# GAT and mean aggregation on one core: one signal for each store of first products, and the first loads of u issued one group later

## Chip, core and metric

The kernel runs on 1 core of one Trainium2 chip. The metric is the time of one execution on the device, in microseconds; less is better.

## What is computed

There are N = 8192 nodes with C = 64 features and a dense 0/1 adjacency matrix of int32 (8192 x 8192, 256 MB). The first block is a normalization, two graph attention layers and a linear layer over the concatenation; the second is a normalization and a mean over the neighbours.

```python
def _gat_layer(h, adj_mask, W_l, lw, lb, a):
    Wh = h @ W_l
    u = Wh @ lw[:C] @ a
    v = Wh @ lw[C:] @ a
    e = leaky_relu(u + v.T + lb @ a, negative_slope=0.2)
    att = softmax(where(adj_mask, e, -9e15), axis=1)
    return elu(att @ Wh)

h0 = maximum(layernorm(x), 0)                      # h = h0
for i in range(2):
    h = 0.2 * h0 + 0.8 * _gat_layer(h, adj > 0, W[i], lin_w[i], lin_b[i], attn[i])
x = x + concatenate([h0, h1, h2]) @ mlp_w + mlp_b
h = maximum(layernorm(x), 0)
a = (adj == 1)
x = x + concatenate([a @ h / a.sum(1), h], 1) @ weight + bias1
```

## The kernel before

**The mathematics as the kernel lays it out.** exp(leaky_relu(u + v)) is, on either side of the kink, a product of a factor of the row and one of the column. So attention becomes two matrix products over 0/1 masks: an on-mask (edge present, u + v positive) and an off-mask (edge present, u + v not positive), each against h times a column factor, split into bf16 or fp16 parts. The masks are bytes read by TensorE as fp8.

**Tiling.** The adjacency is cut into 64 blocks n = 8 g + c: g is a group of 1024 rows, c a chunk of 1024 columns. A block comes in two loads m = 2 n and 2 n + 1 of 2 MB each (line 285, on SyncE's queue, into 3 buffers); VectorE's conversion m (line 852, `convert`) turns load m from int32 into codes, then packs four columns into a byte (lines 859 and 866), TensorE transposes the packed codes (line 1495), ScalarE takes them from PSUM (line 468) and stores them in DRAM (line 472, `codes_d`), so that the second attention layer and the mean need not read the adjacency again. Load m is issued when conversion m - 3 is done.

**Units.** A block has four units; unit U = 256 l + 4 n + q, with l the attention layer and q one of the four bit places. For each unit ScalarE writes two ramps (line 460, `ramps`) from the row of u (buffer `ub`) into `onb[U % 8]`, VectorE makes the on-mask in place (line 830) and the off-mask in `offb[U % 6]` (line 840), and TensorE multiplies both (lines 1505 and 1511). VectorE runs three blocks ahead with its conversions; inside block n its order is written out by hand: on-mask 0, on-mask 1, off-mask 0, conversion 2 (n + 3), off-mask 1, on-mask 2, conversion 2 (n + 3) + 1, off-mask 2, and so on, in the first group with a part of the split of the next chunk's h in between. Conversions 0 to 5 stand ahead of block 0.

**The start.** Before block 0, for each group k of rows, TensorE multiplies h0 with the weights (line 1463), ScalarE takes h W into `hw` (line 425) and h0 times the first part of `mlp_w`, the first products, into `m0[k]` (line 426), and VectorE takes v and u (line 644). The eight buffers `m0[k]`, 2 KB for each partition, lie in the memory of the mask rings: `m0[0]` to `m0[5]` in `offb[0]` to `offb[5]`, `m0[6]` and `m0[7]` in `onb[6]` and `onb[7]`. They must be in DRAM (`m0_d`) before a mask is written there.

**GpSimd's queue** issues the stores and small loads in program order. `store_u(k)` (line 322) writes the 1024 values of u of group k to DRAM, 4 KB in pieces of 8 bytes; `load_u(k)` (line 329) reads them back to all 128 partitions (512 KB) and first waits until the store of u of that parity has landed; line 345 stores `m0[k]`; `load_h0` (line 335) loads h0. An issuing engine that waits holds back all that stands behind it in its queue.

**The waits in question.** `m0_st` is one semaphore that every store of first products raises by 16 when it lands. Before unit 0's off-mask VectorE waits for 128, and before unit 6's ramps ScalarE does, which is for all eight.

Of the kernel before, what the change touches and what calls it, by code (L numbers as in the profile page):

```python
# [32 lines left out]
NG = N // RG  # L33
# [19 lines left out]
NA, NP, NS, NO = 3, 4, 8, 6  # L53
# [3 lines left out]
def word(bits):  # L57
    return bits * 0x01010101


def w32(buf):
    return buf.bitcast(U32)
# [24 lines left out]
def gnn_program(nc, x, adj, w, lin_w, lin_b, attn, mlp_w, mlp_b, w1, bias1, out):  # L87
    ctx = ExitStack()
    with ctx:
# [3 lines left out]
        def sem(name):  # L93
            return ctx.enter_context(nc.semaphore(name))
# [4 lines left out]
        m0_d = nc.dram_tensor("m0_d", (P, T * C), FP32).ap()  # L99
# [51 lines left out]
        def at(off, n, dt):  # L151
            return region[:, off:off + n].bitcast(dt)
# [8 lines left out]
        m0 = [at(78 * KB + 2 * ((k + 2) % 8) * KB, 2 * KB, FP32).rearrange("p (t c) -> p t c", c=C) for k in range(NG)]  # L161
# [35 lines left out]
        def grp(k):  # L197
            return slice(IT * k, IT * k + IT)
# [4 lines left out]
        def dgrp(d, k):  # L203
            return d.rearrange("p (t c) -> p t c", c=C)[:, grp(k), :]

        def pairs(ap):
            return ap.rearrange("p (q b) c -> p q (b c)", b=2)
# [15 lines left out]
        s_cen, s_sq, hn_r, hi0_r, cat0_r, h0_st = (sem("centred"), sem("squares"), sem("h0_ready"), sem("h0_high"), sem("h0_split"),  # L223
                                                   sem("h0_stored"))
        h_r, hi_r, cat_r = sem("h_ready"), sem("h_high"), sem("h_split")
        m0_st, m_st = sem("m0_stored"), [sem(f"m1_stored{i}") for i in range(2)]
        tT, hT_r, mm_done, mm_out, mm_v, d_r = (sem("h_transposed"), sem("ht_ready"), sem("products"), sem("products_taken"),
                                                sem("products_taken_by_vector"), sem("v_u_ready"))
        u_r, bv_r, w_first = sem("u_ready"), sem("v_scaled"), sem("first_tiles_split")
# [37 lines left out]
        with nc.Block() as block:  # L267
# [35 lines left out]
            def _(pool):  # L303
# [15 lines left out]
                def store_u(X):  # L319
                    l, k = X // NG, X % NG  # L320
                    pool.wait_ge(u_r, 3 * X + 3 if l == 0 else 2 * NG + X + 1)
                    pool.dma_start(u_v[l, k], vu[:, 1, grp(k)].rearrange("p (q b) -> p q b", b=2)).then_inc(u_st[X % 2], 16)  # L322

                def load_u(G):
                    pool.wait_ge(u_st[G % 2], 16 * 4 if 2 <= G < NG else 16 * (G // 2 + 1))
                    if G >= 2:
                        pool.wait_ge(sgn, 4 * NCH * (G - 1))
                    l, g = G // NG, G % NG
                    pool.dma_start(ub[G % 2][:, :], u_d[l, g * RG:(g + 1) * RG].partition_broadcast(P)).then_inc(ub_in[G % 2], 16)

                def load_h0(E):
                    pool.wait_ge(h0_st, 16 * 4)
                    if E >= 2:
                        pool.wait_ge(h_r, E - 1)
                    pool.dma_start(hg[E % 2][:, :, :], dgrp(h0_d, E % NG)).then_inc(hg_in[E % 2], 16)
# [3 lines left out]
                    pool.dma_start(h0_d.rearrange("p (t c) -> p t c", c=C)[:, quarter(k), :], hn[:, quarter(k), :]).then_inc(h0_st, 16)  # L339
                for k in range(NG):  # L340
                    store_u(k)
                    if k < 2:
                        load_u(k)
                    pool.wait_ge(mm_out, 3 * k + 3)
                    pool.dma_start(dgrp(m0_d, k), m0[k]).then_inc(m0_st, 16)
                load_h0(0)
                load_h0(1)
                for e in range(NG):
# [11 lines left out]
                def load_x(e):  # L360
                    if e == 0:
                        pool.wait_ge(d_r, 2 * NG)
                        pool.wait_ge(m0_st, 16 * NG)
                        for i in range(2):
                            pool.wait_ge(m_st[i], 16 * NG // 2)
                    else:
                        pool.wait_ge(xm_r, e)
                    pool.dma_start(pairs(xi[e % 2]), xin_v[e]).then_inc(xi_in[e % 2], 16)
                    pool.dma_start(xg[0], dgrp(m0_d, e)).then_inc(xg_in[0], 16)
                    pool.dma_start(xg[1], dgrp(m1_d, e)).then_inc(xg_in[1], 16)  # L370

                def store_base(e):
                    pool.wait_ge(base_r, e + 1)
                    pool.dma_start(dgrp(base_d, e), x2b[e % 2]).then_inc(base_st[e % 2], 16)

                load_x(0)
                for e in range(NG):
                    if e + 2 < NG:
                        load_u(NG + e + 2)
                    if e >= 2:  # L380
                        store_base(e - 2)
                    if e + 1 < NG:
                        load_x(e + 1)
                    if e + 2 < NG:
                        load_h0(NG + e + 2)
# [10 lines left out]
            def _(act):  # L396
# [45 lines left out]
                def ramps(l, n, q):  # L442
                    U = LU * l + 4 * n + q
                    g, c = n // NCH, n % NCH
                    G = NG * l + g
                    if U >= NS:
                        act.wait_ge(on_done, U - NS + 1)
                        act.wait_ge(off_r, U - NS + 1)
                    elif U == NS - 2:
                        act.wait_ge(m0_st, 16 * NG)  # L450
                    if q == 0 and c == 0:
                        act.wait_ge(ub_in[G % 2], 16 * (G // 2 + 1))
                    if q == 0 and g == 0 and l == 0:
                        act.wait_ge(bv_r, 1)
                    if q == 0 and g == 0 and l == 1:
                        act.wait_ge(d_r, NG + c + 1)
                    sv = onb[U % NS].rearrange("k (i b) -> k b i", b=2)
                    for b in range(2):
                        t = c * TC + 2 * q + b
                        last = nc.scalar.activation(sv[:, b, :], ub[G % 2][:, :], ACT.Relu, bias=bigv[l][:, t:t + 1], scale=BIG)  # L460
                    last.then_inc(sgn, 1)
# [66 lines left out]
                for n in range(NT):  # L528
                    g, r = n // NCH, n % NCH
                    ramps(0, n, 0)  # L530
                    if g == 0 and r > 0:
                        cast_high(0, r)
                    ramps(0, n, 1)
                    if n + 1 < NT:
                        take_codes(n + 1)
                    if r == 5 and g > 0:
                        high(NG + g - 1)
                    ramps(0, n, 2)
                    if n + 1 < NT:
                        store_codes(n + 1)  # L540
                    if g == 0 and r > 0:
                        cast_middle(0, r)
                    ramps(0, n, 3)
                    if g > 0 and r == 7:
                        products(NG + g - 1, 0, tpb)
                    if g > 1 and r < 2:
                        products(NG + g - 2, r + 1, tpb)
                    if g > 0 and r == 0:
                        scaled_sums(g - 1)
                    if g > 0 and r == 3:  # L550
                        row_exp(g - 1)
                    if g > 0 and r == 6:
                        take_ht(NG + g - 1, tpb)
# [32 lines left out]
            def _(dve):  # L586
# [246 lines left out]
                def off_mask(l, n, q):  # L833
                    U = LU * l + 4 * n + q
                    if U >= NO:
                        dve.wait_ge(off_done, U - NO + 1)
                    elif U == 0:
                        dve.wait_ge(m0_st, 16 * NG)
                    dve.wait_ge(on_r, U + 1)
                    nc.vector.scalar_tensor_tensor(w32(offb[U % NO]), w32(pt[(NT * l + n) % NP]), word(BITS[q]), w32(onb[U % NS]),  # L840
                                                   ALU.bitwise_and, ALU.bitwise_xor).then_inc(off_r, 1)
# [178 lines left out]
                for n in range(NT):  # L1020
# [5 lines left out]
                    on_mask(0, n, 0)  # L1026
                    on_mask(0, n, 1)
                    off_mask(0, n, 0)
                    if n + 1 < NCH:
                        split_rest(0, n + 1)  # L1030
                    if ahead:
                        convert(n + 3, 0)
                    off_mask(0, n, 1)
                    if g > 0 and r == 1:
                        add_pairs(g - 1)
# [17 lines left out]
                    if n == 1:  # L1053
                        h_spread(0)
                    off_mask(0, n, 2)
                    if g > 0 and r == 1:
                        lonely_add(g - 1)
# [731 lines left out]
```

## Time and profile before

| What | Value |
|---|---|
| median of 3 runs | 1750.88 us (1749.9 to 1751.87) |
| the profiled execution's own time | 1752.64 us |
| its span | 1750.7 us |
| mean granted TensorE clock | 0.971 of full speed |
| busy, share of the span | TensorE 88%, weight loads 85%, VectorE 88%, ScalarE 73%, GpSimd 5% |
| DMA | 356.01 MB, mean 203 GB/s |

Busy shares are a mean over stages with different limits: up to about 850 us the adjacency is read and the first attention layer runs; then the second attention layer, up to about 1500 us; then the mean over neighbours. Times of instructions count from the span's start. In the timeline "x4" is four instructions merged into one row, and the bracket at a row's end is the idle time before it and what ended it. A time to landing runs from a DMA's issue to its last signal. "DMA share" is the mean busy share of the 16 DMA engines; it can read slightly over 1.

### The profile page before, as it was taken

The page shows a single profiled execution, that of the slowest core. Times are in us where ns is not written, and L with a number is a line of the kernel's source. Part 1 is how long each engine was busy: PE and PEld are TensorE (multiplying, and loading weights), DVE is VectorE, ACT ScalarE, POOL GpSimd, SP SyncE. Part 2 cuts the span into 40 slices and gives each one's busy share as a digit, 9 for nine tenths or more (in the row PEclk, how much of TensorE's full clock was granted, in tenths as well). Part 3 has the DMA queues.
Part 4 walks back from the last instruction along what each step waited for, and adds up shares of the span by engine and source line. Part 5 has one row for each costly group of instructions (what it writes and reads, how often), then busy time and mean ns, then how long its engine had stood idle before and what let it go on. Part 6 is the DMA issues. An engine that isn't in the chain of part 4 may idle for free. (4 is left out here: it accounts for less than half of the span.)

```text
span 1750.7 us, 50197 instructions
## 1 busy us (share of the span) xinstructions
PE 1534.7 (88%) x21779; PEld 1489.1 (85%) x21779; DVE 1533.0 (88%) x2473; ACT 1274.4 (73%) x1411; POOL 89.7 (5%) x124
## 2 busy tenths in 40 slices
PE   2358888888988888888779999999999999799998
PEld 2257778888878878787779999999999999799998
DVE  7789999999999999999788877879688788986665
ACT  3758798989888888889689999999999994000000
POOL 1300000101000010101010000000000000000000
PEclk9679999999999999999889999999999999999999
DMA  7988999999999999998121211122121111233231
GB/s 275 286 306 322 375 364 396 348 410 372 409 385 392 388 384 403 361 410 303 54 51 44 56 43 56 44 68 62 38 62 48 52 54 27 62 116 86 88 93 42
DMA packets 114876, 356.01 MB, mean 203 GB/s; under 512 B 9184, under 2 KB 17376, under 8 KB 114656
## 3 DMA queue, kind: packets, MB, share of 16 engines
q1 hardware_dynamic: 91040, 304.27, 46.5%
q0 software_dynamic: 9152, 29.43, 6.2%
q10 hardware_dynamic: 14464, 19.11, 3.3%
q8 instruction: 171, 2.80, 0.7%
q14 instruction: 49, 0.40, 0.1%
HBM read 325.45 MB, written 27.33 MB: 202 GB/s over the span
## 5 line engine op out<-in xcount | busy, mean ns | idle before, releaser
L460 ACT ACTIVATE region<-ub,bigv 128x1024 uint8<-128x1024 f32 x1024 | 1096.0, 1151 | 38.9 <-PE bank L1511 11.2
L1505 PE MATMUL bank<-wsplit,region 128*128 128x195 bf16 x8192 | 786.5, 250 | 43.9 <-DVE region L830 35.6
L1505 PEld LDWEIGHTS bank<-wsplit,region 128*128 128x128 fp8e3 x8192 | 693.2, 99 | 56.3 <-DVE region L830 37.2
L1511 PE MATMUL bank<-wsplit,region 128*128 128x130 f16 x8192 | 556.4, 221 | 66.7 <-DVE region L840 65.2
L1511 PEld LDWEIGHTS bank<-wsplit,region 128*128 128x128 fp8e3 x8192 | 499.3, 98 | 93.0 <-DVE region L840 89.1
L840 DVE SCALAR_TENSOR_TENSOR region<-region 128x512 uint32<-128x512 uint32 x512 | 338.7, 681 | 22.7 <-DMA m_d<-region 13.3
L830 DVE SCALAR_TENSOR_TENSOR region<-region 128x512 uint32<-128x512 uint32 x512 | 334.4, 681 | 10.8 <-ACT region L460 10.7
L852 DVE TENSOR_SCALAR region<-region 128x4096 uint8<-128x4096 int32 x128 | 292.1, 2282 | 0.6 <-DMA region<-in_adj 0.6
L1718 PE MATMUL bank<-wsplit,region 128*128 128x129 f16 x4096 | 243.5, 222 | 11.1 <-DVE region L1337 11.1
L1718 PEld LDWEIGHTS bank<-wsplit,region 128*128 128x128 fp8e3 x4096 | 241.4, 99 | 12.4 <-DVE region L1337 12.3
L1337 DVE TENSOR_SCALAR region<-region 128x512 uint32<-128x512 uint32 x256 | 100.2, 423 | 43.0 <-PE bank L1718 37.6
L468 ACT ACTIVATE region<-bank 128x1024 uint16<-128x1024 uint16 x64 | 65.9, 1030 | 38.2 <-PE bank L1495 38.2
L859 DVE SCALAR_TENSOR_TENSOR region<-region 128x1024 uint32<-128x1024 uint32 x64 | 77.7, 1214 | 0.0
L1495 PE MATMUL bank<-identb,region 128*128 128x128 bf16 x512 | 40.6, 224 | 24.7 <-DVE region L866 14.6
L1463 PE MATMUL bank<-w,hT 128*128 128x130 f16 (+2 forms) x512 | 36.7, 222 | 20.1 <-ACT hT L417 11.6
L1495 PEld LDWEIGHTS bank<-identb,region 128*128 128x128 bf16 x512 | 32.4, 100 | 25.3 <-DVE region L866 14.9
L1463 PEld LDWEIGHTS bank<-w,hT 128*128 128x128 f16 x512 | 30.2, 102 | 22.3 <-issue 12.5
L322 POOL DMA_DIRECT2D u_d<-vu x16 | 14.2, 889 | 662.8 <-DVE vu L662 658.1
L1326 DVE SCALAR_TENSOR_TENSOR region<-region 128x512 uint32<-128x512 uint32 x64 | 43.7, 682 | 0.0
L866 DVE SCALAR_TENSOR_TENSOR region<-region 128x512 uint32<-128x512 uint32 x64 | 43.5, 680 | 0.1
L903 DVE TENSOR_REDUCE parts<-bank 128x130 f32<-128x390 f32 x36 | 20.0, 563 | 26.3 <-PE bank L1505 24.1
L495 ACT ACTIVATE po<-po 128x512 f32<-128x512 f32 x16 | 10.0, 627 | 42.9 <-DVE po L952 42.7
(193 smaller groups left out, 677.2 us busy)
## 6 DMA issues: line engine op xcount, KB each, us to landing
region<-in_adj SPq DMA_DIRECT2D x128, 2048.0 KB, 10.9
region<-codes_d SPq DMA_DIRECT2D x128, 256.0 KB, 2.7
codes_d<-region ACTq DMA_DIRECT2D x64, 256.0 KB, 6.3
ub<-u_d POOLq DMA_DIRECT2D x16, 512.0 KB, 8.2
hg<-h_d POOLq DMA_DIRECT2D x16, 256.0 KB, 6.3
stg<-m_d POOLq DMA_DIRECT2D x16, 256.0 KB, 5.0
region<-in_x SPq DMA_DIRECT2D x4, 512.0 KB, 6.8
h_d<-wsplit POOLq DMA_DIRECT2D x4, 512.0 KB, 4.2
```

Of the source, the lines that this page charges most:

```text
L460: last = nc.scalar.activation(sv[:, b, :], ub[G % 2][:, :], ACT.Relu, bias=bigv[l][:, t:t + 1], scale=BIG)
L468: nc.scalar.activation(pt[n % NP].bitcast(U16), tpb[:, :].bitcast(U16), ACT.Copy).then_inc(p_in, 1)
L830: nc.vector.scalar_tensor_tensor(on, on, word(BITS[q]), w32(pt[(NT * l + n) % NP]), ALU.bitwise_and, ALU.bitwise_and).then_inc(on_r, 1)
L840: nc.vector.scalar_tensor_tensor(w32(offb[U % NO]), w32(pt[(NT * l + n) % NP]), word(BITS[q]), w32(onb[U % NS]), ALU.bitwise_and, ALU.bitw ...
L852: nc.vector.tensor_scalar(code[:, 4 * h:4 * h + 4, :], adjb[m % NA], 1.375, 3.0, ALU.mult, ALU.min).then_inc(coded, 1)
L859: nc.vector.scalar_tensor_tensor(cq[:, :, :, 0, :], cq[:, :, :, 1, :], 2, cq[:, :, :, 0, :], ALU.logical_shift_left, ALU.bitwise_or).then_ ...
L1337: nc.vector.tensor_scalar(w32(onb[V % NS]), w32(xb[i % 2]), word(BITS[q]), None, ALU.bitwise_and).then_inc(eq, 1)
L1463: last = nc.tensor.matmul(pb[:, k * width:(k + 1) * width], ht[:, it * P:(it + 1) * P], rhs(j), start=(k == 0 and j == 0), stop=(j == 1), ...
L1495: last = nc.tensor.transpose(tpb[:, :].bitcast(BF16)[:, it * P:(it + 1) * P], src[:, it, :], identb[:, :])
L1505: return nc.tensor.matmul(acc_on[it], columns(onb[U % NS], it, b), wsplit[:, c * TC + 2 * q + b, 0:WC], start=(c == 0 and q == 0 and b == ...
L1511: return nc.tensor.matmul(acc_off[it], columns(offb[U % NO], it, b), woff[:, c * TC + 2 * q + b, WO:WO + WF], start=(c == 0 and q == 0 and ...
L1718: last = nc.tensor.matmul(acc_m[g % 2][it], columns(onb[V % NS], it, b), wf16[:, c * TC + 2 * q + b, :], start=(first and b == 0 and it % ...
```

## The change

The one semaphore for the stores of first products becomes eight, one for each store. Before unit U's first use of its ring buffer there is now a wait for store U alone: on VectorE for units 0 to 5 (off-masks), on ScalarE for units 6 and 7 (ramps). Where GpSimd waited for all eight before it reads them back, `load_x(0)`, it waits for each in turn. The two first loads of u leave their place between the store of u and the store of products of groups 0 and 1; they now stand at the end of groups 1 and 2.

```diff
@@ -223,7 +223,7 @@
         s_cen, s_sq, hn_r, hi0_r, cat0_r, h0_st = (sem("centred"), sem("squares"), sem("h0_ready"), sem("h0_high"), sem("h0_split"),
                                                    sem("h0_stored"))
         h_r, hi_r, cat_r = sem("h_ready"), sem("h_high"), sem("h_split")
-        m0_st, m_st = sem("m0_stored"), [sem(f"m1_stored{i}") for i in range(2)]
+        m0_st, m_st = [sem(f"m0_stored{k}") for k in range(NG)], [sem(f"m1_stored{i}") for i in range(2)]
         tT, hT_r, mm_done, mm_out, mm_v, d_r = (sem("h_transposed"), sem("ht_ready"), sem("products"), sem("products_taken"),
                                                 sem("products_taken_by_vector"), sem("v_u_ready"))
         u_r, bv_r, w_first = sem("u_ready"), sem("v_scaled"), sem("first_tiles_split")
@@ -339,10 +339,10 @@
                     pool.dma_start(h0_d.rearrange("p (t c) -> p t c", c=C)[:, quarter(k), :], hn[:, quarter(k), :]).then_inc(h0_st, 16)
                 for k in range(NG):
                     store_u(k)
-                    if k < 2:
-                        load_u(k)
                     pool.wait_ge(mm_out, 3 * k + 3)
-                    pool.dma_start(dgrp(m0_d, k), m0[k]).then_inc(m0_st, 16)
+                    pool.dma_start(dgrp(m0_d, k), m0[k]).then_inc(m0_st[k], 16)
+                    if 1 <= k < 3:
+                        load_u(k - 1)
                 load_h0(0)
                 load_h0(1)
                 for e in range(NG):
@@ -360,7 +360,8 @@
                 def load_x(e):
                     if e == 0:
                         pool.wait_ge(d_r, 2 * NG)
-                        pool.wait_ge(m0_st, 16 * NG)
+                        for k in range(NG):
+                            pool.wait_ge(m0_st[k], 16)
                         for i in range(2):
                             pool.wait_ge(m_st[i], 16 * NG // 2)
                     else:
@@ -446,8 +447,8 @@
                     if U >= NS:
                         act.wait_ge(on_done, U - NS + 1)
                         act.wait_ge(off_r, U - NS + 1)
-                    elif U == NS - 2:
-                        act.wait_ge(m0_st, 16 * NG)
+                    elif U >= NO:
+                        act.wait_ge(m0_st[U], 16)
                     if q == 0 and c == 0:
                         act.wait_ge(ub_in[G % 2], 16 * (G // 2 + 1))
                     if q == 0 and g == 0 and l == 0:
@@ -834,8 +835,8 @@
                     U = LU * l + 4 * n + q
                     if U >= NO:
                         dve.wait_ge(off_done, U - NO + 1)
-                    elif U == 0:
-                        dve.wait_ge(m0_st, 16 * NG)
+                    else:
+                        dve.wait_ge(m0_st[U], 16)
                     dve.wait_ge(on_r, U + 1)
                     nc.vector.scalar_tensor_tensor(w32(offb[U % NO]), w32(pt[(NT * l + n) % NP]), word(BITS[q]), w32(onb[U % NS]),
                                                    ALU.bitwise_and, ALU.bitwise_xor).then_inc(off_r, 1)
```

## Rows read from the trace of the kernel before

**Rows 1.** Long stretches: busy of PE, PEld, DVE, ACT, POOL; PEclk, DMA share, GB/s.
```profile
96.00:846.00 750.00, 643.24 (x8588) 604.67 (x8587) 748.10 (x885) 651.65 (x760) 28.12 (x25) 0.98 0.96 367
...
900.00:1450.00 550.00, 548.63 (x7815) 548.19 (x7813) 448.82 (x830) 522.40 (x501) 27.00 (x38) 1.00 0.18 52
```
**Rows 2.** VectorE's waits from 96 to 860 us: in total, times, longest.
```profile
DVE region L852 <- DMA region<-in_adj: 0.6, 1, 0.6
```
**Rows 3.** Waits of all engines up to 130 us: in total, times, longest.
```profile
DVE region L840 <- DMA m_d<-region: 13.3, 1, 13.3
...
ACT region L460 <- DMA m_d<-region: 10.3, 1, 10.3
```
**Rows 4.** Timeline of VectorE and ScalarE, 58 to 111 us: start, duration, engine, line.
```profile
58.94 0.48 DVE L644 TENSOR_SCALAR vu<-bank,wsc 128x6 f32<-128x6 f32 x3
...
64.96 2.28 DVE L852 TENSOR_SCALAR region<-region 128x4096 uint8<-128x4096 int32 x1
...
65.49 4.25 ACT L460 ACTIVATE region<-ub,bigv 128x1024 uint8<-128x1024 f32 x4
...
74.11 2.28 DVE L852 TENSOR_SCALAR region<-region 128x4096 uint8<-128x4096 int32 x1
...
79.52 1.28 DVE L830 SCALAR_TENSOR_TENSOR region<-region 128x512 uint32<-128x512 uint32 x2
...
94.06 0.69 DVE L840 SCALAR_TENSOR_TENSOR region<-region 128x512 uint32<-128x512 uint32 x1 [13.26 <-DMA m_d<-region]
...
98.70 0.68 DVE L830 SCALAR_TENSOR_TENSOR region<-region 128x512 uint32<-128x512 uint32 x1
...
99.30 2.28 DVE L852 TENSOR_SCALAR region<-region 128x4096 uint8<-128x4096 int32 x1
...
110.08 2.28 DVE L852 TENSOR_SCALAR region<-region 128x4096 uint8<-128x4096 int32 x1
```
**Rows 5.** Timeline of GpSimd's queue: loads of u, last store of first products.
```profile
48.82 0.54 POOL L329 DMA_DIRECT2D ub<-u_d  x1 [7.62 <-DMA u_d<-vu]
...
61.12 0.54 POOL L329 DMA_DIRECT2D ub<-u_d  x1 [8.38 <-DMA u_d<-vu]
...
71.37 0.71 POOL L345 DMA_DIRECT2D m_d<-region  x1
```
**Rows 6.** Issues and landings: adjacency, first products, stores of u, first load of u.
```profile
L285 SPq DMA_DIRECT2D region<-in_adj x3: 368/368/368, 45.9 to 56.9; - x3
DMA to landing us min/median/max: 11.3/12.8/22.3
...
L285 SPq DMA_DIRECT2D region<-in_adj x1: 368/368/368, 67.3 to 67.3; - x1
DMA to landing us min/median/max: 26.7/26.7/26.7
...
L345 POOL DMA_DIRECT2D m_d<-region x8: 540/541/2642, 49.3 to 71.4; - x8
DMA to landing us min/median/max: 8.2/16.3/22.7
...
L322 POOL DMA_DIRECT2D u_d<-vu x8: 757/758/2798, 40.4 to 70.6; - x8
DMA to landing us min/median/max: 8.1/17.1/22.4
...
DMA to landing us min/median/max: 7.9/7.9/7.9
```
**Rows 7.** Short stretches: DMA share and GB/s are the last two columns.
```profile
44.00:52.00 8.00, 4.49 (x72) 4.02 (x72) 7.97 (x14) 8.00 (x25) 3.18 (x3) 1.00 0.84 299
56.00:64.00 8.00, 3.05 (x21) 2.12 (x19) 7.18 (x25) 3.40 (x10) 2.88 (x5) 0.52 1.04 351
68.00:92.00 24.00, 3.80 (x24) 3.00 (x24) 12.42 (x26) 13.03 (x14) 5.15 (x9) 0.57 1.04 215
104.00:108.00 4.00, 2.24 (x35) 1.97 (x33) 3.91 (x7) 0.83 (x2) 0.00 (x0) 1.00 1.02 413
```

## The prediction, made before the change was run

> **What bounds the kernel now.** I read the time in three stretches and asked of each whether an earlier start would reach the end. From 96 us to 846 us VectorE is busy 748.10 of 750 us [rows 1]; it is the only engine that is full, and it waits there only once, for 0.6 us, for adjacency data [rows 2]. From 900 to 1450 us TensorE is busy 548.63 of 550 us [rows 1]. Each stretch starts where the one before it ends, so time won on VectorE before 96 us should be there at the end, unless something that VectorE reads is late. The only long hole is just before: VectorE waits 13.3 us for the DMA that stores the first products, ScalarE 10.3 us for the same [rows 3]. In the timeline the hole runs from 80.80 us (end of the two on-masks of unit 0 and 1) to 94.06 us, where the first off-mask starts [rows 4]. The last store of first products was issued at 71.4 us and took 22.7 us to land [rows 5, 6], which is 94.1 us: the wait is for store 7, although the buffer wanted is that of store 0.
>
> **Part 1: one signal for each store.** The first off-mask then needs store 0 alone. That was issued at 49.3 us in the kernel as it is and landed 8.2 us later [rows 6], and it is issued earlier still below; it cannot be late for 80.80 us. So the 13.26 us of this wait go. ScalarE's unit 6 needs store 6, VectorE's units 1 to 5 need stores 1 to 5. The waits added (five on VectorE, one on ScalarE at another unit, seven on GpSimd's queue for a load hundreds of microseconds later) are met before they are reached, and I cost them at nothing: where waits are met, as ahead of the conversion at 99.30 us, it follows the mask of 98.70 us after 0.60 us, less than the mask's own 0.68 us [rows 4]. Were store 6 late, ScalarE would stand with the store of codes and the middle cast behind it, and VectorE would want them only some 10 us later.
>
> **Part 2: the loads of u one group later.** GpSimd's queue stands 7.62 us at the first load of u and then 8.38 us at the second, each time until the store of u just issued has landed [rows 5]. Everything behind is late: eight products are taken by 59.4 us [rows 4], but stores 1 to 7 are issued after 61.12 us, the last at 71.37. After the change, stores 0 and 1 go out before the first wait: store 0 behind the store of u at 40.4 us (0.76 us) [rows 6], store 1 some 3 us later, when the next products are taken. The first load of u goes at 48.8 us as now, since it waits for the same landing. The second follows the stores of u 2 and of products 2, at about 51 to 52 us instead of 61.12. From there nothing holds the queue but the products: the last store is issued at about 60.2 us, 11 us earlier. An issue takes 0.54 us, or 2.64 us, it seems where it meets one of VectorE's conversions [rows 6]; even three such meetings cost only 6 us of a queue that nobody waits for any more. ScalarE reads the first load of u only at 65.49 us [rows 4], and it lands at 56.7 (48.82 + 7.9) [rows 5, 6]. With the change stores 0 and 1 of products and one of u stand ahead of it, 2.6 us or so of DMA work; the cover is 8.8 us, and the on-masks that read the ramps come at 79.52 us only [rows 4].
>
> **What is late next.** After the hole VectorE does an off-mask, the rests of a split, conversion 6 of the adjacency, an off-mask, an on-mask and conversion 7, which starts at 99.30 us, 5.24 us after the hole's end [rows 4]. Without a hole that is 80.80 + 5.24 = 86.04 us. Conversion 7 needs the adjacency tile whose load was issued at 67.3 us and took 26.7 us [rows 6]: it is there at 93.9 us. So the DMA engines, hidden until now behind the wait, come last. (The three loads before it, issued at 45.9, 51.9 and 56.9 us, took 11.3, 12.8 and 22.3 us in that order [rows 6].) Conversion 6 at about 82.6 us needs the tile of 56.9 + 22.3 = 79.2 us.
>
> Can that tile land earlier? From 68 to 92 us the 16 engines are fully busy but move 215 GB/s, where 413 GB/s is what they reach at 104 to 108 us; before, at 56 to 64 us with one store of u among it, they move 351 [rows 7]. The slow stretch holds the six last stores of u, and ends as the last of these lands (issued at 70.6 us, 22.4 us later, 93.0) [rows 6]. Each of them writes 4 KB in pieces of 8 bytes. Lost are (1 - 215/413) x 24 = 11.5 us, or 1.9 us for each of the six. The change neither removes a store nor makes one cheaper. It only starts them earlier, so what counts is how much idle DMA time there is to start them in. Between 44 and 52 us the DMA share is 0.84 [rows 7], so 1.3 us are idle; from 52 us on there is none to speak of. Against it the store of the third codes, now held back to 94.07 us by the same wait on ScalarE, moves ahead of the tile: 256 KB at 413 GB/s is 0.6 us. So the tile lands at 93.9 - 1.3 + 0.6 = 93.2 us. Then conversion 7 starts at 93.3 us instead of 99.30: **6.0 us won**, and 7.3 us of the hole come back as a new wait in front of line 852.
>
> The Trainium skill speaks against this pricing: by "DMA: Bandwidth & Descriptors", section "Anatomy of one DMA", a DMA takes about 2.0 us plus its bytes over 436 GB/s, which for the 2 MB tile gives an estimate of 6.8 us and would leave no wait at all. The trace does not agree (26.7 us for that tile); the same page's specifications say that pieces under 512 bytes are written by read-modify-write, with which the slow stretch agrees.
>
> Two more needs. Conversion 5, at 74.11 us [rows 4], uses the tile that lands at 64.7 us (51.9 + 12.8) [rows 6]. The stores of u now compete with its load and the one before. Where they compete, successive tiles land 14.5 and 14.7 us apart (64.7, 79.2, 93.9) [rows 6]. Tile 4 lands at 57.2 us (45.9 + 11.3) [rows 6]; with the stores beside it I put it at about 62 us (conversion 4 reads it at 64.96 us [rows 4]), and that pace puts tile 5 at 77 us: a wait of 3 us at conversion 5, but from there to conversion 7 VectorE has 99.30 - 74.11 - 13.26 = 11.9 us of work, so it gets there at 89 us, still ahead of 93.2. Conversion 8, now at 110.08 us [rows 4], comes at 104 us; its tile is next in the queue, and 2 MB at 413 GB/s take 5.1 us, which is 98.3 us. Later loads are issued when VectorE frees a buffer and move with it.
>
> **Sum.** The profiled execution took 1752.64 us, with a span of 1750.7 us and 1.9 us around it; a profiled execution like it would take 1752.6 - 6.0 = 1746.6 us. The median of the runs, 1750.88, lies 1.8 us below it; on that scale the forecast is 1744.9 us.
> Bounds of this case: if no idle time can be used and the codes' store is in front, the tile lands at 94.5 us, and with 0.5 us of lag the gain is 4.3 us. If stores of u that come singly cost less, as in 56 to 64 us, where (1 - 351/413) x 8 = 1.2 us were lost for one [rows 7], six save 0.7 us each and the gain is 10.2 us.
>
> **Rivals.**
> *The whole hole is won.* The slow stretch has another cause than the stores of u (their crowding behind the late queue, say), the tile lands before 86 us, and the gain is 13.3 us: 1737.6 us. For it speaks that tiles land in 12.8 us and less before the crowd [rows 6]; against it, that the slowness ends with the last store of u, and that nothing is taken from the DMA engines' work. The skill's byte formula above would give this result. Chance 0.09.
> *Nearly nothing is won.* Tile 5 is starved by the stores that now run beside it: if it lands later than 83.9 us, VectorE comes to conversion 7 later than 95.8 us and the gain is under 3.5 us; a gain of 2 us gives 1748.9 us. For it speaks the pace of 14.7 us and a tile 4 that could be starved as well; against it, that the queue holds only six more stores of u, all done by 80 us or so. A second way to the same time is that tile 7 lands at 96 us because the mixture is less efficient. Also here belongs that the change does not do what it says, that is, the waits resolve no earlier than now: 1750.9. Chance 0.17.
> *Slower.* The same mechanism farther on: VectorE reaches conversion 7 later than 99.30 us if tile 5 lands after 87.4 us, that is if tiles 4 and 5 come 19 us apart instead of 14.7. Tile 5 at 91.5 us would cost 4.1 us: 1755.0 us. The skill, "DMA: Bandwidth & Descriptors", section "Queues, rings and completion order", has a rule that points this way: a DMA's signal lands only after every earlier write of its engine, of any queue, and the writes put ahead of tile 5's signal are the slow ones. No row here can show this by itself. Chance 0.04.
>
> **Numbers.** The forecast has 0.70. A measurement of this kernel can tell about 0.2%, 3.5 us, from no change. Faster by more: 0.70 + 0.09 = 0.79; within: 0.17; slower: 0.04. The range runs from 1740.0 (a gain of 10.9 us, the cheap stores of u and a little of the first rival) to 1748.2 us (2.7 us, the upper part of the second).
>
> **What would show it.** Right: no wait on a store of products anywhere, VectorE's first off-mask at 80.8 us (or up to some 5 us later, behind conversion 5), the last store of products issued by 60 to 64 us, conversion 7 waiting for the adjacency's DMA until 92 to 94.5 us, and all that follows shifted by 5 to 7 us. Wrong: conversion 7 without a wait; a longer wait at conversions 4 or 5; or new waits for adjacency after 100 us that give the gain back.

## The result

The changed kernel takes 1746.32 us (median of 12 runs, 1744.54 to 1748.78), where the kernel before takes 1750.83 us in the same sets (12 runs, 1749.62 to 1754.67): a ratio of 0.9973, 95% interval 0.9965 to 0.9981, or 4.7 us (3.3 to 6.1). The profiled execution took 1748.78 us with a span of 1746.7 us, where that of before had 1750.7.

The place of the wait is where the gain is read. First the waits of VectorE and, below, its timeline in the changed kernel (lines have moved down by one: 841 is the off-mask, 853 the conversion):

```profile
DVE region L853 <- DMA region<-in_adj: 9.9, 3, 3.9
```

```profile
77.47 2.30 DVE L853 TENSOR_SCALAR region<-region 128x4096 uint8<-128x4096 int32 x1 [3.87 <-DMA region<-in_adj]
...
84.10 0.68 DVE L841 SCALAR_TENSOR_TENSOR region<-region 128x512 uint32<-128x512 uint32 x1
...
89.84 2.30 DVE L853 TENSOR_SCALAR region<-region 128x4096 uint8<-128x4096 int32 x1 [3.84 <-DMA region<-in_adj]
...
95.52 2.29 DVE L853 TENSOR_SCALAR region<-region 128x4096 uint8<-128x4096 int32 x1 [2.18 <-DMA region<-in_adj]
```

No instruction waits for a store of products any more. The hole of 13.26 us of [rows 4] has become three waits for adjacency, 9.9 us together: at conversions 5, 6 and 7, with 3.87, 3.84 and 2.18 us. The first off-mask starts at 84.10 us in place of 94.06, conversion 7 at 95.52 in place of 99.30. Of a hole of 13.3 us, 3.4 us are won. Conversion 7 is 3.8 us earlier; the rest, 0.4 us, is a lead that this execution had before the change could act: GpSimd's first store, ahead of all edited lines, goes out at 25.80 us instead of 26.31, and conversion 4 starts at 64.44 us instead of 64.96.

GpSimd's queue is as forecast; its second load of u and its last store of products (rows of its timeline) now go out at 52.76 and 61.12 us, where [rows 5] had 61.12 and 71.37:

```profile
52.76 0.54 POOL L329 DMA_DIRECT2D ub<-u_d  x1
...
61.12 0.54 POOL L343 DMA_DIRECT2D m_d<-region  x1
```

The adjacency's loads of tiles 5 to 8 (tile m is the one that conversion m reads). In each pair of rows the first has the moment of issue, behind the three durations of the issue in ns, and the second the time to landing:

```profile
L285 SPq DMA_DIRECT2D region<-in_adj x1: 368/368/368, 51.4 to 51.4; - x1
...
DMA to landing us min/median/max: 26.0/26.0/26.0
...
L285 SPq DMA_DIRECT2D region<-in_adj x1: 368/368/368, 56.5 to 56.5; - x1
...
DMA to landing us min/median/max: 33.4/33.4/33.4
...
L285 SPq DMA_DIRECT2D region<-in_adj x1: 368/368/368, 66.8 to 66.8; - x1
...
DMA to landing us min/median/max: 28.7/28.7/28.7
...
L285 SPq DMA_DIRECT2D region<-in_adj x1: 368/368/368, 79.8 to 79.8; - x1
...
DMA to landing us min/median/max: 20.8/20.8/20.8
```

Tile 5 lands at 77.4 us, tile 6 at 89.9, tile 7 at 95.5 and tile 8 at 100.6. In [rows 6] tiles 5, 6 and 7 landed at 64.7, 79.2 and 93.9 us. Tile 8 had this row in the kernel before, which is also 100.6 us:

```profile
L285 SPq DMA_DIRECT2D region<-in_adj x1: 368/368/368, 76.4 to 76.4; - x1
...
DMA to landing us min/median/max: 24.2/24.2/24.2
```

So tile 8 lands when it did, and the tiles before it are dealt out differently: the change gave the transfers another order. It is not quite the same work: from 44 to 100.6 us the engines moved 306 GB/s, where before they moved 286, but none of that brought tile 8 forward. The stretches show the new order (DMA share and GB/s are the last two columns):

```profile
44.00:84.00 40.00, 11.26 (x127) 9.27 (x124) 34.04 (x82) 27.74 (x58) 15.66 (x18) 0.62 1.01 263
...
68.00:92.00 24.00, 6.75 (x56) 6.07 (x56) 15.98 (x27) 17.36 (x20) 0.00 (x0) 0.59 1.00 294
...
84.00:104.00 20.00, 13.09 (x136) 12.17 (x133) 13.89 (x18) 10.53 (x13) 0.00 (x0) 0.82 1.02 409
```

and the last store of u, with issue and time to landing:

```profile
L322 POOL DMA_DIRECT2D u_d<-vu x1: 757/757/757, 60.4 to 60.4; - x1
...
DMA to landing us min/median/max: 23.9/23.9/23.9
```

From 68 to 92 us the rate is 294 GB/s where [rows 7] had 215, since the stores of u are now over at 84.3 us; they slow the engines earlier instead, to 263 GB/s from 44 to 84 us (290 before).

What follows is shifted and otherwise as it was. VectorE is full to 842 us, then TensorE:

```profile
96.00:842.00 746.00, 637.97 (x8537) 598.90 (x8538) 744.62 (x882) 646.72 (x754) 27.96 (x25) 0.98 0.96 368
896.00:1446.00 550.00, 549.27 (x7824) 548.98 (x7822) 448.84 (x829) 522.40 (x500) 27.00 (x38) 1.00 0.17 52
```

From the start of conversion 7 to the end of the span are 1651.2 us here and 1651.4 us before.

### The profile page after: what moved, and what is told of

The parts are those of the page before. It is cut to its first block and busy times, and to the rows that moved or that the text cites. A ratio compares the mean times of both kernels' runs of the same rounds, so it can differ in the third digit from the quotient of the medians.

```text
span 1746.7 us, 50205 instructions
## 1 busy us (share of the span) xinstructions
PE 1533.3 (88%) x21779; PEld 1486.9 (85%) x21779; DVE 1533.1 (88%) x2473; ACT 1274.0 (73%) x1411; POOL 91.5 (5%) x124
## 6 DMA issues: line engine op xcount, KB each, us to landing
region<-in_adj SPq DMA_DIRECT2D x128, 2048.0 KB, 11.1
```

## The experiments

The kernel before was timed again beside each set, because its time differs from set to set, each on one chip of its own: 1750.8, 1756.8, 1752.3 and 1755.7 us. So every kernel is compared by its ratio to the kernel before on its own chip. The last two columns are read from each kernel's own trace.

| Kernel | set, before us | us | ratio (95%) | conversion 7 starts | from there to the end |
|---|---|---|---|---|---|
| before (first profile) | 1750.8 | | | 99.30 | 1651.4 |
| before, again | 1752.3 | | | 98.00 | 1650.6 |
| changed | 1750.8 | 1746.3 | 0.9973 (0.9965 to 0.9981) | 95.52 | 1651.2 |
| changed, again | 1752.3 | 1747.0 | 0.9971 (0.9959 to 0.9982) | 95.11 | 1651.2 |
| signals alone | 1756.8 | 1751.1 | 0.9966 (0.9954 to 0.9978) | 97.70 | 1651.2 |
| loads of u alone | 1756.8 | 1751.1 | 0.9966 (0.9954 to 0.9978) | 96.50 | 1651.5 |
| changed, late stores of u | 1756.8 | 1741.5 | 0.9912 (0.9899 to 0.9925) | 86.43 | 1654.4 |
| the same, again | 1755.7 | 1740.2 | 0.9909 (0.9896 to 0.9923) | 86.42 | 1652.7 |
| before, late stores of u | 1752.3 | 1739.1 | 0.9926 (0.9913 to 0.9940) | 85.83 | 1651.7 |
| the same, again | 1755.7 | 1742.0 | 0.9922 (0.9908 to 0.9936) | 87.19 | 1652.7 |
| changed, u in wider pieces | 1752.3 | 1739.0 | 0.9925 (0.9912 to 0.9937) | 85.85 | 1650.8 |
| changed, stores of u twice | 1756.8 | 1763.3 | 1.0036 (1.0023 to 1.0049) | 108.46 | 1651.1 |
| changed, stores of products twice | 1755.7 | 1756.9 | 1.0008 (0.9999 to 1.0017) | 103.61 | 1651.8 |

Over a spread of 22 us in the start of conversion 7, the rest of the span stays within 1650.6 and 1651.8 us in all but three, and these three have small new waits for adjacency later on (2.6, 1.4 and 1.8 us in all). In these traces, time won or lost before conversion 7 reaches the end one to one. Each trace is one execution, and the executions of the kernel before lie up to 3.3 and 5.1 us apart in two of the sets: conversion 7 is earlier by 3.8 us in the first pair of traces and by 2.9 us in the second, where the ratios say 4.7 and 5.1 us.

### Each part of the change alone

The signals alone are the changed kernel with this edit:

```diff
+                    if k < 2:
+                        load_u(k)
                     pool.wait_ge(mm_out, 3 * k + 3)
...
-                    if 1 <= k < 3:
-                        load_u(k - 1)
```

and the moved loads alone are the kernel before with the opposite one:

```diff
-                    if k < 2:
-                        load_u(k)
...
+                    if 1 <= k < 3:
+                        load_u(k - 1)
```

Expected of the signals alone: 

> One signal for each store of first products, the loads of u left where they were. Theory (the hole's end passes to the DMA engines' work): no wait on a store at the first off-mask; the adjacency tiles land as before, tile 5 at about 65 us, tile 6 at 79, tile 7 at 94 to 94.5, so conversion 7 starts near 94.3 us instead of 99.3: 5 us won, 1745.8 us, as much as with both parts. Rival (the moved loads carry the gain): the stores' crowd after 61 us stays, and without part 2 little is won: under 2 us, 1749 us or more.

Expected of the loads alone: 

> The loads of u issued one group later, one signal for all stores as before. Theory: the last store of first products lands at about 85 us, and VectorE, which waits for tile 5 until 77 us, gets to its first off-mask at 84 us: a wait of at most 1 us, then tiles 6 and 7 at 90 and 95.5 us as in the changed kernel; 4 to 4.5 us won, 1746.5 us. Rival (the eight signals carry the gain): a wait of several microseconds stays at the first off-mask and under 2 us are won.

VectorE's conversions in the kernel with the signals alone:

```profile
84.32 2.29 DVE L853 TENSOR_SCALAR region<-region 128x4096 uint8<-128x4096 int32 x1 [1.96 <-DMA region<-in_adj]
...
97.70 2.29 DVE L853 TENSOR_SCALAR region<-region 128x4096 uint8<-128x4096 int32 x1 [9.88 <-DMA region<-in_adj]
```

and in the kernel with the moved loads alone:

```profile
80.88 2.29 DVE L852 TENSOR_SCALAR region<-region 128x4096 uint8<-128x4096 int32 x1 [6.58 <-DMA region<-in_adj]
...
90.81 2.29 DVE L852 TENSOR_SCALAR region<-region 128x4096 uint8<-128x4096 int32 x1 [1.39 <-DMA region<-in_adj]
...
96.50 2.29 DVE L852 TENSOR_SCALAR region<-region 128x4096 uint8<-128x4096 int32 x1 [2.19 <-DMA region<-in_adj]
```

Both give 0.9966, and their intervals overlap widely with those of the two parts together (0.9973 and 0.9971). Each part alone wins what the two win, and each rival, by which one part carries the gain, falls. With the signals alone the hole becomes one wait of 9.88 us at conversion 7 and 1.96 us at conversion 6. With the moved loads alone VectorE waits 6.58 us for tile 5, and by the time it comes to the first off-mask, at 87.51 us, all eight stores have landed, the last one at 87.5 us; there is no wait for them. In both, tile 7 is the gate. With the signals alone one of the new waits does show: the last stores of products are still issued after 71 us, and ScalarE waits 11.1 us for the one of unit 6, until 94.63 us. That is off the path, since VectorE waits for tile 7 longer still. A size was off: tile 7 lands at 97.7 us with the signals alone, not at 94.3. The changed kernel was not run on that chip, so how much of these 3.4 us is the chip's is not known.

### The stores of u taken out of the start

```diff
                 for k in range(NG):
-                    store_u(k)
+                    if k < 2:
+                        store_u(k)
                     pool.wait_ge(mm_out, 3 * k + 3)
...
                 load_h0(1)
+                for k in range(2, NG):
+                    pool.wait_ge(coded, 2 * k + 6)
+                    store_u(k)
```

This is the edit of the changed kernel; the kernel before got the same one, with its loads of u left in place. Groups 2 to 7 of u are needed only when their row groups come: the load of group 2 was issued at 175 us in this kernel.

Expected, on the changed kernel: 

> The changed kernel, but the stores of u of groups 2 to 7 are issued one for each block from block 1 on (each waits for a conversion), not before block 0. Theory (six stores of u cost 1.9 us of all DMA engines each): tile 7 lands at about 84 us, before VectorE wants it, conversions 5 to 8 have no wait, conversion 7 at 86 us, and the whole hole is won: 13 us, 1737.6 us. Rival (the slow stretch is the crowd of all stores and loads together, or the adjacency loads themselves): tile 7 still lands after 90 us, 8 us won or less, or the late stores make new waits of 1 us and more at later conversions.

Expected, on the kernel before: 

> The kernel before (one signal for all stores of first products, loads of u in their old place), with the stores of u of groups 2 to 7 issued one for each block from block 1 on. Theory: six stores of u fewer in the DMA engines before 94 us; the last store of first products lands at about 80 to 83 us, so the first off-mask waits at most 2 us, tile 7 lands before 86 us, and 11 to 13 us are won although the change itself is absent. Rival (the one signal or GpSimd's queue is what costs): a wait of 5 us or more stays at the first off-mask and under 8 us are won.

The changed kernel with late stores of u, conversion 7 and the stretch that was slow:

```profile
86.43 2.29 DVE L857 TENSOR_SCALAR region<-region 128x4096 uint8<-128x4096 int32 x1
```

```profile
68.00:92.00 24.00, 11.88 (x125) 11.06 (x126) 23.52 (x40) 20.36 (x22) 0.00 (x0) 0.64 1.02 402
```

The kernel before with late stores of u:

```profile
85.83 2.29 DVE L855 TENSOR_SCALAR region<-region 128x4096 uint8<-128x4096 int32 x1
```

```profile
68.00:92.00 24.00, 12.48 (x136) 11.65 (x137) 23.62 (x38) 19.76 (x21) 0.90 (x2) 0.65 1.01 406
```

The rate in the slow stretch goes from 215 GB/s (259 in the second trace of the kernel before) to 402 and 406, no conversion up to number 8 waits, and conversion 7 starts where VectorE's own work puts it. The prediction's 86.04 us for a start without a hole is met within 0.4 us. The second of these kernels has none of the change in it: one signal for all eight stores, loads of u in the old place. It wins 13.2 us, where the change wins 5.3 us on the same chip.

On top of late stores of u the change is worth little. Both kernels were run again on one chip.

Expected: 

> The changed kernel with late stores of u once more, to stand on one chip beside the next. Expected 12.5 to 14 us under the kernel before; the wait of 2.6 us for adjacency near 750 us, seen once, should be absent or elsewhere if it was chance.

> The kernel before with late stores of u once more, same chip. If the DMA work alone sets the hole's end, the change adds nothing on top of the late stores: within 1 us of the other. If the eight signals still help, it is 1 us or more slower.

With the change, VectorE's conversion 7:

```profile
86.42 2.29 DVE L857 TENSOR_SCALAR region<-region 128x4096 uint8<-128x4096 int32 x1
```

Without it, the first off-mask and conversion 7:

```profile
81.95 0.69 DVE L843 SCALAR_TENSOR_TENSOR region<-region 128x512 uint32<-128x512 uint32 x1 [0.84 <-DMA m_d<-region]
...
87.19 2.29 DVE L855 TENSOR_SCALAR region<-region 128x4096 uint8<-128x4096 int32 x1
```

Without it a wait of 0.84 us for the products' stores stays, and conversion 7 is 0.8 us later. The times are 1740.2 and 1742.0 us, ratios 0.9909 and 0.9922 with intervals that overlap: 1.8 us apart, more than the 1 us I had allowed, with the traces accounting for 0.8 us of it. That the eight signals still help here is likely, not shown. The wait of 2.6 us for adjacency, near 720 us in the first run of this kernel, was not there in the second, which had two waits of 1.4 us together. Where the adjacency's loads run near 400 GB/s all the time, such small waits seem to fall now here, now there; the kernel before had one of 0.6 us [rows 2]. The changed kernel with late stores of u would be the version to keep: 15 us under the kernel before on the two chips where it ran.

### What a store of u costs, and why

Three edits of the changed kernel. Each store of u of groups 2 to 7 twice, 512 pieces of 8 bytes more for each:

```diff
                     store_u(k)
+                    if k >= 2:
+                        pool.dma_start(u2_v[0, k], vu[:, 1, grp(k)].rearrange("p (q b) -> p q b", b=2)).then_inc(u2_st, 16)
```

The same stores in 128 pieces of 32 bytes (the kernel does not read u back in this new order, so in groups 2 to 7 its first layer works with other rows' values; the amount of work is the same):

```diff
+                    if l == 0 and k >= 2:
+                        pool.dma_start(u_d.rearrange("l (g p t) -> l g p t", g=NG, p=P)[l, k], vu[:, 1, grp(k)]).then_inc(u_st[X % 2], 16)
```

Each store of products of these groups twice (the masks then also wait for the second stores):

```diff
+                    if k >= 2:
+                        pool.dma_start(dgrp(m2_d, k), m0[k]).then_inc(m2_st, 16)
```

Expected of the doubled stores of u: 

> The changed kernel with each of the stores of u of groups 2 to 7 issued twice, the second into a scratch tensor (4 KB each, in pieces of 8 bytes): 24 KB more to write. Theory: each takes 1.9 us of the DMA engines, tile 7 lands 11 us later, at about 107 us, and the kernel takes 1757.5 us, 7 us more than before the change. Rival (a store costs its bytes and the queue's 0.76 us): 1747 us, less than 1 us more than the changed kernel.

Expected of the wider pieces: 

> The changed kernel, with the stores of u of groups 2 to 7 written in pieces of 32 bytes instead of 8 (one for each partition, 128 in place of 512, the same 4 KB); the values of u lie in another order in DRAM, so the ramps of groups 2 to 7 of the first attention layer belong to other rows, with no effect on the work done. Theory, cost by piece: a store costs 0.5 us in place of 1.9, tile 7 lands about 8.5 us earlier, at 87 us, and the time is 8 us under the changed kernel's. Rival, cost by store whatever its pieces: tile 7 stays at 95 us and the time within 1 us of the changed kernel's.

Expected of the doubled stores of products: 

> The changed kernel with the stores of first products of groups 2 to 7 issued twice, the second into a scratch tensor: 1.5 MB more to write in wide pieces, 64 times the bytes that the doubled stores of u added. Theory (pieces cost, bytes cost only 256 KB at 413 GB/s, 0.63 us each): tile 7 lands 3.8 us later and the time is 3.8 us over the changed kernel's, about 1750.5 us where the kernel before takes 1751 to 1752. Rival (any added store on this queue costs 1.9 us): 11 us more, as with the doubled stores of u.

With each store of u twice, VectorE's conversions 5 to 7 and the stretch:

```profile
83.64 2.29 DVE L860 TENSOR_SCALAR region<-region 128x4096 uint8<-128x4096 int32 x1 [8.94 <-DMA region<-in_adj]
...
101.49 2.29 DVE L860 TENSOR_SCALAR region<-region 128x4096 uint8<-128x4096 int32 x1 [9.32 <-DMA region<-in_adj]
...
108.46 2.29 DVE L860 TENSOR_SCALAR region<-region 128x4096 uint8<-128x4096 int32 x1 [3.48 <-DMA region<-in_adj]
```

```profile
68.00:92.00 24.00, 3.15 (x22) 2.73 (x23) 14.58 (x31) 12.21 (x14) 1.74 (x4) 0.50 1.05 165
```

24 KB more in the queue, and the engines fall to 165 GB/s, tile 7 comes 12.9 us later than in the changed kernel, and the kernel is slower than before by 0.36%. Against the changed kernel's ratio that is (1.0036 - 0.9973) x 1751 = 11.0 us, 1.8 us for each of the six; 11 us had been expected. The two ratios come from two chips: on the chip of this kernel each half of the change took 1751.1 us, 12.2 us less, or 2.0 us for each, and by the two conversions it is 12.9 us, or 2.2. That a store costs its bytes and its place in the queue, the rival, is out.

With pieces of 32 bytes, conversion 7, the load of its tile, and the stretch:

```profile
85.85 2.29 DVE L856 TENSOR_SCALAR region<-region 128x4096 uint8<-128x4096 int32 x1
```

```profile
L285 SPq DMA_DIRECT2D region<-in_adj x1: 368/368/368, 67.2 to 67.2; - x1
...
DMA to landing us min/median/max: 15.0/15.0/15.0
```

```profile
68.00:92.00 24.00, 11.84 (x135) 10.99 (x136) 23.62 (x38) 19.77 (x21) 0.00 (x0) 0.68 1.01 400
```

The same 4 KB in a quarter of the pieces, and the slow stretch is gone: 400 GB/s. Tile 7 lands at 82.2 us, 12.9 us earlier than in the changed kernel on the same chip (95.1), where I had expected 8.5 us. A store of u in such pieces costs next to nothing, less than the quarter that a price by the piece would give. The time is 8.0 us under that of the changed kernel on the same chip; more cannot be won there, since VectorE is at its own pace.

With the stores of products twice, the conversion and the stretch:

```profile
103.61 2.29 DVE L861 TENSOR_SCALAR region<-region 128x4096 uint8<-128x4096 int32 x1 [3.93 <-DMA region<-in_adj]
```

```profile
68.00:92.00 24.00, 6.48 (x56) 5.81 (x56) 14.66 (x31) 13.53 (x15) 0.00 (x0) 0.55 1.02 227
```

VectorE waits for adjacency alone here; ScalarE waits 7.6 us for the stores, off the path. Six stores of 256 KB in wide pieces cost 8.1 us by the traces and (1.0008 - 0.9973) x 1751 = 6.1 us by the ratios, 1.0 to 1.35 us each: less than 1.9 us, so the rival is out, and more than their bytes at 413 GB/s (0.63 us). How much more is uncertain. The changed kernel was not run on this chip, and from the nearest ends of the two intervals (0.9999 and 0.9981) the cost is 3.2 us, which the 3.8 us expected would fit. In the kernels with late stores of u the eight plain stores of products run in a stretch of more than 400 GB/s and show no such surcharge. So bytes that share the engines with the 8-byte pieces may pay too; whether they do, and why, is open.

## Why the prediction was right, and where it was off

*The bound and the way to the end.* Right. The gain at conversion 7 is the gain in the span, in every trace of the table, but for the small later waits of three.

*Part 1 and the waits added.* Right. The wait for all eight stores was the hole, and in the changed kernel none of the new waits shows. But the prediction gave the 13.26 us to part 1 and treated part 2 as what feeds it. The runs show either part alone to be enough: each brings VectorE to tile 7 before tile 7 has landed, and tile 7 leaves 4 to 6 us of the 13.

*Part 2.* Right in its times: last store issued at 61.1 us (60.2 foreseen, and up to 64 allowed), second load of u at 52.8 us (51 to 52). The cover of the first load of u was thinner than it said: put at 56.7 us and 2.6 us more, it landed at 62.4 us (issued at 49.24, 13.2 us), and ScalarE's ramps read it at 64.97.

*What is late next.* The step on which the forecast rested, that the adjacency's tile 7 lands only with the DMA engines' work, is right, and so is the price of 1.9 us for a store of u: 1.8 to 2.2 us measured by doubling. The conversion without a hole, 86.04 us, is right too. The term that was mis-sized is the tile's landing: 95.5 us, not 93.2. It was built as 93.9 - 1.3 + 0.6. Two things were off in it.

The 1.3 us of idle DMA time brought nothing. The DMA share from 44 to 52 us did rise, from 0.84 to 0.96, and yet tile 8 landed at 100.6 us in both kernels. A tile has landed when the last of its sixteen signals is in: those of tile 8 came from 93.0 to 100.6 us in the kernel before, from 95.3 to 100.6 us in the changed one. The share is a mean over the engines, and it can be low while a tile is still waited for, as in this row of the kernel before:

```profile
98.00:100.00 2.00, 2.00 (x17) 1.91 (x15) 2.00 (x4) 2.00 (x3) 0.00 (x0) 0.50 0.71 217
```

So idle time in the mean need not be time that brings a tile forward. Without that term the tile is put at 94.5 us.

The other 1.0 us has a candidate that the sum left out: the two loads of h0, 256 KB each, that stand last in GpSimd's queue at the start. First the kernel before, then the changed one:

```profile
L335 POOL DMA_DIRECT2D hg<-h_d x2: 542/543/544, 72.1 to 72.6; - x2
...
DMA to landing us min/median/max: 23.4/23.9/24.3
...
L335 POOL DMA_DIRECT2D hg<-h_d x2: 542/543/544, 61.7 to 62.2; - x2
...
DMA to landing us min/median/max: 24.7/25.2/25.7
```

In the kernel before they landed at 95.5 and 96.9 us, behind tile 7; now they land at 86.4 and 87.9 us, ahead of it. At 413 GB/s they are 1.3 us, less what had been moved of them by 94 us before; that would put tile 7 between 94.5 and 95.8 us. No run moves these loads alone, so this is worked out and not shown.

*The two places that lean on the Trainium skill.* Its formula in "DMA: Bandwidth & Descriptors", section "Anatomy of one DMA", is given for DMAs that GpSimd issues, while the adjacency's loads are issued by SyncE; so the estimate of 6.8 us, against 26.7 us measured, stretches it. The Specifications of the same page say that below 512 bytes the DMA engines do read-modify-write, and the prediction found the slow stretch in agreement with that. The pieces of 32 bytes lie below 512 as well, and their stretch runs at 400 GB/s, so the agreement said nothing about the price. Whether the price of 8 bytes lies in the writing or in the number of pieces is separated by no run here.

*The two more needs.* Tile 4 was put at about 62 us and caused no wait at conversion 4; that holds (62.5 us). Tile 5 was put at 77 us with a wait of 3 us; it landed at 77.4 with a wait of 3.9 us. I then left tile 6 at its old 79.2 us. With tile 5 at 77 us that could not be: at the pace of 14.5 us used one line before, tile 6 had to come near 91 us, and it came at 89.9, with a wait of 3.84 us that the prediction did not have. It cost nothing at the end only because tile 7 came later than both.

*Rivals.* "The whole hole is won" fell as a result, but every kernel without the 8-byte stores shows that it was 13 us that stood there to be won. "Nearly nothing" needed tile 5 after 83.9 us, "slower" after 87.4 us. With the stores of u doubled tile 5 came at 83.6 us, tile 7 at 108.4 us, and the kernel was slower than before: what decides is how much slow work stands ahead of tile 7, not tile 5 alone. The condition given for "slower" is also mis-summed: from tile 4 at 62 us to tile 5 at 87.4 us are 25 us, not 19.

*The number.* 6.0 us forecast, 4.7 us (3.3 to 6.1) measured, 1746.3 us inside 1740.0 to 1748.2. Two of its own signs of being right lie just outside: conversion 7 waits until 95.5 us, not 92 to 94.5, and all that follows is shifted by 3.8 us in the traces, not 5 to 7.

## What to carry to other kernels

When a wait goes, ask which transfer was due to land just behind it: if the DMA engines were full during the wait, moving transfers earlier only reorders them, and the next reader takes over the wait. Price the DMA engines by rate, not by share: a stretch with share 1.0 and half of the usual GB/s holds work that its bytes do not show, and taking that out (or only out of the way, as here by a wait for a later block) won 13.2 us where the change won 5.3 on the same chip. When one landing in a chain is moved, carry its delay to the next ones before saying which is last.

## What the hardware showed

A store of 4 KB in 512 pieces of 8 bytes set the DMA traffic back by 1.8 to 2.2 us (an estimate from the doubled stores) while the engines were loaded; the same 4 KB in 128 pieces of 32 bytes cost too little to see. It shows as a low rate at a full DMA share, and in the packets beside it. These are the packets, MB and share of the 16 engines' time of q1, the queue that the adjacency's loads take, from 68 to 92 us; first in the kernel before, then in the kernel before with late stores of u:

```profile
q1 hardware_dynamic: 722, 2.86, 59.5%
...
q1 hardware_dynamic: 1712, 6.80, 70.6%
```

These packets have about 4 KB in both. One took 316 ns in the mean with the 8-byte stores in flight (0.595 x 16 x 24 us / 722) and 158 ns without them. So the delay is recorded in other transfers' packets and not only in those of the stores.

The price is not the same in every execution. On another chip the trace of the kernel before has a hole of 11.46 us in place of 13.26, and 259 GB/s in the slow stretch where [rows 7] has 215:

```profile
92.77 0.69 DVE L840 SCALAR_TENSOR_TENSOR region<-region 128x512 uint32<-128x512 uint32 x1 [11.46 <-DMA m_d<-region]
```

```profile
68.00:92.00 24.00, 3.81 (x24) 3.00 (x24) 12.84 (x26) 13.28 (x14) 5.90 (x10) 0.50 1.04 259
```

The changed kernel has it the other way round, 294 GB/s in the first trace and 272 on that chip, so whether the chip or the execution makes the difference is open. Nor do the times tell whether this stall is behind their spread: the kernel before took 1750.8 to 1756.8 us in the four sets, the kernels with late stores of u or wide pieces 1739.0 to 1742.0, but these ran on fewer chips each, and the kernel before with late stores of u, the same program, took 1739.1 us on one chip and 1742.0 on another. Its five runs ranged over 1.2 us on the first of these and over 6.1 us on the second.
